# Experts weight their rows by the gates and scatter with addition into one row per token

## The chip, the cores and the metric

The kernel runs on one core of a Trainium2 chip. The metric is the time of one execution on the device, in microseconds (us). The core has five engines that run side by side and wait for each other by semaphores: PE (TensorE, matrix products), DVE (VectorE) and ACT (ScalarE) for work on tiles, POOL (GpSimd), which here also issues the indirect DMAs, and SP, which issues the plain ones. A tile has 128 partitions. All DMAs share the core's 16 DMA engines.

## The reference, cut to what matters

Two layers, each `x = x + s * silu(f)`. The change touches the second layer's f, a mixture of 8 experts of which each token takes 2:

```python
logits = xt @ wg                                   # xt: 8192 tokens x 256
scores = softmax(logits);  topv, topi = top_k(scores, 2)
topv = topv / sum(topv)
pos = running number of each (k, token) within its expert     # k = 0 first
valid = pos < capacity                             # capacity 2 * 8192 / 8 = 2048
gate = topv * valid
disp[topi, pos] = xt                               # the rows of each expert
h = relu(disp @ w1 + b1)                           # 256 -> 1024
y = h @ w2 + b2                                    # 1024 -> 256
f = sum over k of gate[k] * y[topi[k], pos[k]]
x = x + s * silu(f)
```

Everything is f32; in the experts the kernel writes each f32 matrix as a sum of two f16 halves and forms three products for one.

## The kernel before

`program` calls the stages `prepare`, `mix`, `recur`, `attend`, `route`, `experts` and `combine`. Each is a block: all engines begin it together and end it together. Within a block the order on each engine is the order in which its program is written; nothing reorders it.

`recur` also clears the DRAM tensor `expert_rows` (`y_dram`, 2 x 8192 rows of 256 f32, one per chosen expert and token) with 16 DMAs of 1 MB from SP, since a (k, token) beyond an expert's capacity gets no row (L684).

`route` finds the two best experts of each token, their gates (`gates`, 128 x 2 x 64), and each token's place in its expert. A loop of 128 steps on POOL, ACT, DVE and PE (L1236 to L1295) builds the table `token`: for each of the 8 x 2048 places of the experts the number of the (k, token) that stands there, plus one, or 0 for an empty place. From it DVE makes `idx`, the row of x to be gathered (L1251), and `dst`, the row of `expert_rows` to be written (L1248).

`experts` goes through 32 groups of 512 places, four (g = 0 to 3) to an expert. The loop of PE, ACT and DVE holds two experts, that of POOL two groups. In group n:

- PE forms h in eight chunks of six matmuls (L1645 to L1647) into four PSUM buffers; ACT takes them out with relu (L1600), DVE forms the lower halves (L1539). Then PE turns the x of group n+1 (L1617) and forms y in 96 matmuls (L1666 to L1668).
- DVE takes y out of PSUM, scales it and adds b2 into `yo` (L1563), which raises `yb_ready`. PE waits for it before it writes y of the next group. In front of that DVE copies the next group's columns of `dst` into `dcol` (`take_dcol`, L1455), for which it waits until the scatter of the group before has landed (`y_out`).
- POOL issues four indirect DMAs that gather the rows of group n+2 (`gather`, L1426), waits for `yb_ready`, and issues four that scatter `yo` to `expert_rows` (L1438), 128 rows of 1 KB each.
- SP loads the weights of the next expert into `raw`.

`combine` takes 16 tiles of 128 tokens x 4 batches x 256. SP loads the two rows of each token, `ya` and `yb` (L1715), six tiles ahead in eight buffers; ACT multiplies `ya` by the first gate (`first`, four instructions, L1782); DVE adds `yb` times the second gate (`add`, four instructions, L1742), ACT forms silu (L1773), DVE multiplies by s (`prod_st`, L1755), POOL adds x (L1765), SP stores (L1723).

## Time and profile before

| | us |
|---|---|
| median of 3 runs (lowest, highest) | 1655.68 (1654.1, 1657.88) |
| profiled execution, its own time | 1656.6 |
| span of the profile | 1654.8 |
| PE, DVE, ACT, POOL busy | 1321.9, 1069.8, 644.6, 608.4 |
| experts, matmuls of the groups (829 to 1551) | 722 |
| combine (from 1563) | 92 |

The span runs from the first to the last instruction. Busy is the time in which an engine executes an instruction of its own; issuing a DMA counts as busy on POOL and not on SP. A wait is put down to the instruction that released it. The average over the whole span says little here, since the stages have different limits.

### The profile page before, as it was taken

How to read it: one execution, taken by the hardware profiler on the slowest of the kernel's cores; microseconds unless marked ns; L12 is line 12 of the kernel's file. 1: busy time of each engine (PE TensorE's matmuls, PEld its weight loads, DVE VectorE, ACT ScalarE, POOL GpSimd, SP SyncE). 2: the span in 40 equal slices, each digit the busy share in tenths (PEclk: the TensorE clock that was granted, in tenths of full speed). 3: DMA queues.
4: the chain of work that ended last, by engine and by line, in shares of the span. 5: the costliest groups of instructions: out<-in, count | busy, mean ns of one | idle time of the engine just before them, and what ended most of it. 6: DMA issues, size and time to landing. Idle time of an engine off the chain costs nothing. (4 is left out here: it accounts for less than half of the span.)

```text
span 1654.8 us, 23701 instructions
## 1 busy us (share of the span) xinstructions
PE 1321.9 (80%) x7637; PEld 904.2 (55%) x7637; DVE 1069.8 (65%) x2021; ACT 644.6 (39%) x947; POOL 608.4 (37%) x567
## 2 busy tenths in 40 slices
PE   0699999668999898335499999999999999999400
PEld 0466666336777776311156676666667665667300
DVE  0677776016999999789855555665455655555398
ACT  0255554222322222125354544454444455454263
POOL 0112121001666666714423433333433333343245
PEclk9899999658999999655599999999999999999755
DMA  8000000811000001010121313121221313122396
GB/s 262 1 0 0 0 0 0 348 59 39 25 25 25 25 28 37 0 51 0 29 80 52 103 46 100 51 83 55 81 71 47 103 42 103 52 93 46 102 319 222
DMA packets 75222, 116.07 MB, mean 70 GB/s; under 512 B 9313, under 2 KB 62371, under 8 KB 73088
## 3 DMA queue, kind: packets, MB, share of 16 engines
q1 hardware_dynamic: 53520, 72.44, 13.2%
q0 software_dynamic: 12720, 33.96, 6.8%
q10 hardware_dynamic: 8896, 8.53, 1.7%
q8 instruction: 54, 0.88, 0.2%
q14 instruction: 32, 0.26, 0.1%
HBM read 65.36 MB, written 50.33 MB: 70 GB/s over the span
## 5 line engine op out<-in xcount | busy, mean ns | idle before, releaser
L1600 ACT ACTIVATE e_h_all<-e_pH,e_b1c,e_h_scale 128x512 f32<-128x512 f32 x256 | 199.8, 781 | 370.9 <-PE e_pH L1647 370.6
L1666 PE MATMUL e_pY<-e_w_hi,e_h_hi 128*128 128x256 f16 x1024 | 279.3, 273 | 5.2 <-DVE e_w_lo L1511 5.2
L1667 PE MATMUL e_pY<-e_w_lo,e_h_hi 128*128 128x256 f16 x1024 | 279.1, 273 | 0.0
L1668 PE MATMUL e_pY<-e_w_hi,e_h_lo 128*128 128x256 f16 x1024 | 279.1, 273 | 0.0
L1426 POOL DMA_INDIRECT e_xg<-xn_rows,e_icol x136 | 154.4, 1135 | 302.0 <-DVE e_icol L1452 260.2
L1539 DVE TENSOR_TENSOR e_h_lo<-e_h_all,e_h_hi 128x512 f16<-128x512 f32 x256 | 177.2, 692 | 108.1 <-ACT e_h_hi L1600 102.1
L1645 PE MATMUL e_pH<-e_x_hi,e_w_hi 128*128 128x512 f16 x512 | 196.5, 384 | 10.2 <-issue 6.4
L1647 PE MATMUL e_pH<-e_x_hi,e_w_lo 128*128 128x512 f16 x512 | 196.6, 384 | 0.0
L1646 PE MATMUL e_pH<-e_x_lo,e_w_hi 128*128 128x512 f16 x512 | 196.5, 384 | 0.0
L1438 POOL DMA_INDIRECT expert_rows<-e_yo,e_dcol x128 | 130.9, 1023 | 151.7 <-DVE e_yo L1563 120.7
L1563 DVE SCALAR_TENSOR_TENSOR e_yo<-e_pY,e_y_scale,logit_st 128x1024 f32<-128x1024 f32 x32 | 41.1, 1283 | 154.4 <-PE e_pY L1668 154.4
L1085 PE MATMUL c_pY<-wqkv,c_xnT 128*128 128x256 f32 x512 | 130.0, 412 | 0.0
L1085 PEld LDWEIGHTS c_pY<-wqkv,c_xnT 128*128 128x128 f32 x512 | 107.8, 211 | 21.4 <-issue 1.1
L1666 PEld LDWEIGHTS e_pY<-e_w_hi,e_h_hi 128*128 128x128 f16 x1024 | 100.2, 98 | 18.6 <-DVE e_h_lo L1539 7.4
L1668 PEld LDWEIGHTS e_pY<-e_w_hi,e_h_lo 128*128 128x128 f16 x1024 | 100.2, 98 | 11.6
L1667 PEld LDWEIGHTS e_pY<-e_w_lo,e_h_hi 128*128 128x128 f16 x1024 | 100.2, 98 | 11.4
L1600 ACT ACTIVATE e_h_hi<-e_pH,e_b1c,e_h_scale 128x512 f16<-128x512 f32 x128 | 99.0, 774 | 0.0
L1645 PEld LDWEIGHTS e_pH<-e_x_hi,e_w_hi 128*128 128x128 f16 x512 | 50.7, 99 | 69.9 <-issue 14.1
L1295 PE MATMUL d_ptab<-d_val,d_ohl 128*128 128x256 f16 x128 | 44.8, 400 | 51.6 <-ACT d_ohl L1276 26.8
L1647 PEld LDWEIGHTS e_pH<-e_x_hi,e_w_lo 128*128 128x128 f16 x512 | 50.6, 99 | 61.9 <-issue 2.7
L1646 PEld LDWEIGHTS e_pH<-e_x_lo,e_w_hi 128*128 128x128 f16 x512 | 50.6, 99 | 57.6 <-issue 2.8
L999 ACT ACTIVATE c_q<-c_pY 128x1024 f32<-128x1024 f32 x16 | 16.4, 1024 | 151.1 <-DVE c_qk L950 141.1
(257 smaller groups left out, 2554.5 us busy)
## 6 DMA issues: line engine op xcount, KB each, us to landing
raw<-L_ffn_w SPq DMA_DIRECT2D x18, 1024.0 KB, 5.9
expert_rows<-r_zero SPq DMA_DIRECT2D x16, 1024.0 KB, 16.7
x_st<-L_attn_x ACTq DMA_DIRECT2D x4, 2048.0 KB, 22.2
xn_rows<-c_xn SPq DMA_DIRECT2D x16, 512.0 KB, 2.9
f_ya<-expert_rows SPq DMA_DIRECT2D x16, 512.0 KB, 5.7
f_yb<-expert_rows SPq DMA_DIRECT2D x16, 512.0 KB, 6.6
out<-f_ya SPq DMA_DIRECT2D x16, 512.0 KB, 3.7
e_xg<-xn_rows,e_icol POOLq DMA_INDIRECT x136, 2.8
```

The costliest lines, as they stand in the source:

```text
L1085: last = pe.matmul(dst[:, b, :], xnT[:, kk, b * P:(b + 1) * P], v.wqkv[:, kk, n * D:(n + 1) * D], start=False, stop=(kk == KD - 1), skip_g ...
L1295: pe.matmul(ptab[:, 0:2 * P], ohl[m][:, u, :], val[u][:, :, :].rearrange("p a b -> p (a b)"), start=False, stop=False, skip_group_check=Tr ...
L1426: pool.indirect_dma_start(xg[u][:, q, :], None, v.xn3_dram, bass.IndirectOffsetOnAxis(icol[u][:, q:q + 1], axis=0), bounds_check=N - 1, oo ...
L1438: pool.indirect_dma_start(v.y_dram, bass.IndirectOffsetOnAxis(dcol[u][:, q:q + 1], axis=0), yo[u][:, q, :], None, bounds_check=TOPK * N - ...
L1539: dve.tensor_tensor(h_lo[:, h, :], h_all[h % 2][:, :], h_hi[:, h, :], ALU.subtract).then_inc(h_lo_ready, 1)
L1600: last = act.activation(dst, pH[h % NPH][:, :], ACT.Relu, bias=b1c[eu][:, h:h + 1], scale=h_scale[eu][:, 0:1])
L1645: pe.matmul(pH[h % NPH][:, :], w1_hi[:, k, rows], x_hi[:, k, :], start=(k == 0), stop=False)
L1646: pe.matmul(pH[h % NPH][:, :], w1_hi[:, k, rows], x_lo[:, k, :], start=False, stop=False)
L1647: last = pe.matmul(pH[h % NPH][:, :], w1_lo[:, k, rows], x_hi[:, k, :], start=False, stop=(k == KD - 1))
L1666: pe.matmul(pY[:, q, :], h_hi[:, h, cols], w2_hi[:, h, :], start=(h == 0), stop=False)
L1667: pe.matmul(pY[:, q, :], h_hi[:, h, cols], w2_lo[:, h, :], start=False, stop=False)
L1668: last = pe.matmul(pY[:, q, :], h_lo[:, h, cols], w2_hi[:, h, :], start=False, stop=(h == HT - 1))
```

## The change

Each expert multiplies its rows by the gates and adds them into one row per token. `expert_sums` has 8192 rows for the tokens and 2048 more, to which the empty places of an expert go (each to a row of its own within one expert). The gates are turned by PE, written to the DRAM tensor `gate_rows`, and gathered by place with `gid` as the index: 512 single values a group. The scatter adds to what is in the row. Because two experts may add to the same row, POOL waits at the end of each expert until all its scatters have landed. `combine` loads one row per token, and ACT begins with silu. The core of the diff (declarations of buffers and semaphores are left out):

```diff
@@ -71,7 +72,8 @@
     c[:, C_P] = np.arange(P) + 1
     c[NS::GRP, C_SAT] = SAT
     c[:, C_E:C_E + E] = np.arange(E)
-    c[:, C_G:] = np.arange(TOPK * NG)
+    c[:, C_G:C_D] = np.arange(TOPK * NG)
+    c[:, C_D:] = N + np.arange(P)[:, None] + P * (np.arange(P) % (CAP // P))
     return c
 
 
...
-    v.y_dram = nc.dram_tensor("expert_rows", [TOPK * N, D], F32, kind="Internal").ap()
+    v.y_dram = nc.dram_tensor("expert_sums", [N + CAP, D], F32, kind="Internal").ap()
+    v.gate_dram = nc.dram_tensor("gate_rows", [TOPK * N, 1], F32, kind="Internal").ap()
...
-                parts = TOPK * N // (P * 8)
+                parts = (N + CAP) // (P * 8)
...
+                sp.wait_ge(gates_taken, 1)
+                sp.dma_start(v.gate_dram.rearrange("(n p) o -> n (p o)", p=P), gate_rows[:, :]).then_inc(gates_out, 16)
+                sp.wait_ge(gates_out, 16)
...
-                for t in (v.idx, v.dst):
+                for t in (v.idx, v.dst, v.gid):
...
-                linked(dve.tensor_tensor(gates[:, 1, :], ee[:, :], gates[:, 0, :], ALU.mult))
+                dve.tensor_tensor(gates[:, 1, :], ee[:, :], gates[:, 0, :], ALU.mult).then_inc(gates_ready, 1)
...
@@ -1237,18 +1249,21 @@
                                           v.cst[:, bass.ds(C_G + n, 1)], ALU.is_equal, ALU.mult)
                         dve.tensor_scalar(val[u][:, 1, :], iota[:, :], hi[:, bass.ds(n, 1)],
                                           v.cst[:, C_P:C_P + 1], ALU.is_equal, ALU.mult).then_inc(one_ready, 1)
+                dve.wait_ge(gates_turned, 1)
+                dve.tensor_copy(gate_rows[:, :], pgate[:, 0:P]).then_inc(gates_taken, 1)
                 dve.wait_ge(table, 1)
                 linked(dve.tensor_copy(tab[:, :, :], ptab[:, 0:2 * P].rearrange("p (a b) -> p a b", a=2)))
 
                 linked(dve.scalar_tensor_tensor(token[:, :], tab[:, 0, :], float(P), tab[:, 1, :], ALU.mult, ALU.add))
 
-                linked(dve.tensor_scalar(empty[:, :], token[:, :], 0.0, None, ALU.is_equal))
-                linked(dve.scalar_tensor_tensor(t1[:, :], empty[:, :], float(TOPK * N + 1), token[:, :],
-                                                ALU.mult, ALU.add))
-                dve.tensor_scalar(v.dst[:, 0:P], t1[:, :], -1.0, None, ALU.add)
+                dve.tensor_scalar(v.gid[:, 0:P], token[:, :], -1.0, 0.0, ALU.add, ALU.max)
+                linked(dve.scalar_tensor_tensor(empty[:, :], token[:, :], 0.0, v.cst[:, C_D:C_D + P],
+                                                ALU.is_equal, ALU.mult))
                 linked(dve.tensor_scalar(t2[:, :], token[:, :], float(N), float(-N), ALU.is_gt, ALU.mult))
                 linked(dve.scalar_tensor_tensor(t2[:, :], t2[:, :], -1.0, token[:, :], ALU.add, ALU.add))
-                linked(dve.tensor_scalar(v.idx[:, 0:P], t2[:, :], 0.0, None, ALU.max))
+                linked(dve.tensor_scalar(t2[:, :], t2[:, :], 0.0, None, ALU.max))
+                dve.tensor_copy(v.idx[:, 0:P], t2[:, :])
+                linked(dve.tensor_tensor(v.dst[:, 0:P], t2[:, :], empty[:, :], ALU.add))
 
             @block.gpsimd
             def _(pool):
...
+                pe.wait_ge(gates_ready, 1)
+                pe.transpose(pgate[:, 0:P], gates[:, :, :].rearrange("p k g -> p (k g)"), v.ident).then_inc(gates_turned, 1)
...
@@ -1427,20 +1449,37 @@
                                                 bass.IndirectOffsetOnAxis(icol[u][:, q:q + 1], axis=0),
                                                 bounds_check=N - 1, oob_is_err=False).then_inc(x_in[u], 16)
 
+                def gather_gates(n, u):
+                    pool.wait_ge(gcols, n + 1)
+                    pool.sem_inc(passed, 1)
+                    for q in range(BLK):
+                        pool.indirect_dma_start(gate[u][:, q:q + 1], None, v.gate_dram,
+                                                bass.IndirectOffsetOnAxis(gcol[u][:, q:q + 1], axis=0),
+                                                bounds_check=TOPK * N - 1, oob_is_err=False).then_inc(gate_in[u], 16)
+
                 for u in range(2):
                     gather(u, u)
-                with pool.Fori(0, NGR // 2) as i:
-                    for u in range(2):
-                        gather(2 * i + u + 2, u)
-                        pool.wait_ge(yb_ready, 2 * i + u + 1 + 1)
+                gather_gates(0, 0)
+                with pool.Fori(0, E) as e:
+                    for g in range(GRPS):
+                        u = g % 2
+                        n = GRPS * e + g
+                        gather(n + 2, u)
+                        gather_gates(n + 1, 1 - u)
+                        pool.wait_ge(weighted, n + 1)
                         pool.sem_inc(passed, 1)
                         for q in range(BLK):
                             pool.indirect_dma_start(
                                 v.y_dram, bass.IndirectOffsetOnAxis(dcol[u][:, q:q + 1], axis=0), yo[u][:, q, :], None,
-                                bounds_check=TOPK * N - 1, oob_is_err=False).then_inc(y_out[u], 16)
+                                bounds_check=N + CAP - 1, oob_is_err=True, compute_op=ALU.add).then_inc(y_out[u], 16)
+                        if g == GRPS - 1:
+                            for m in range(2):
+                                pool.wait_ge(y_out[m], 8 * BLK * GRPS * (e + 1) + 16 * m)
                 for u in range(2):
                     pool.wait_ge(y_out[u], 16 * BLK * NGR // 2 + 16 * u)
                     pool.wait_ge(x_in[u], 16 * BLK * (NGR // 2 + 1))
+                pool.wait_ge(gate_in[0], 16 * BLK * (NGR // 2 + 1))
+                pool.wait_ge(gate_in[1], 16 * BLK * NGR // 2)
 
             @block.vector
             def _(dve):
...
+                    dve.tensor_copy(gcol[u][:, :], v.gid[:, bass.ts(n, BLK)]).then_inc(gcols, 1)
...
@@ -1563,6 +1603,11 @@
                     dve.scalar_tensor_tensor(yo[u][:, :, :], pY[:, :, :], y_scale[eu][:, 0:1],
                                              b2b[eu].unsqueeze(1).broadcast_to([P, BLK, D]),
                                              ALU.mult, ALU.add).then_inc(yb_ready, 1)
+                    dve.wait_ge(gate_in[u], 8 * BLK * (n - u) + 16 * BLK)
+                    dve.wait_ge(yb_ready, n + 2)
+                    dve.tensor_tensor(yo[u][:, :, :], yo[u][:, :, :],
+                                      gate[u][:, :].unsqueeze(2).broadcast_to([P, BLK, D]),
+                                      ALU.mult).then_inc(weighted, 1)
 
                 groups(dve, body)
 
...
-                rows = v.y_dram.rearrange("(k b t p) d -> t k p b d", k=TOPK, b=B, p=P)
+                rows = v.y_dram[0:N, :].rearrange("(b t p) d -> t p b d", b=B, p=P)
...
-                    for k, y in enumerate((ya[n], yb[n])):
-                        sp.dma_start(y[:, :].rearrange("p (b d) -> p b d", b=B), rows[t, k]).then_inc(y_in[n], 16)
+                    sp.dma_start(ya[n][:, :].rearrange("p (b d) -> p b d", b=B), rows[t]).then_inc(y_in[n], 16)
...
@@ -1731,26 +1772,19 @@
                 for n in range(NB):
                     sp.wait_ge(o_out[n], 16 * (NT // NB) + 16)
 
+            @block.scalar
+            def _(act):
+                def body(i, n, left):
+                    act.wait_ge(y_in[n], 16 * (i + 1))
+                    act.sem_inc(passed, 1)
+                    act.activation(ya[n][:, :], ya[n][:, :], ACT.Silu).then_inc(silu_ready, 1)
+
+                rounds(act, body)
+
             @block.vector
             def _(dve):
-                def add(i, n):
-                    t = NB * i + n
-                    dve.wait_ge(y_in[n], 32 * (i + 1))
-                    dve.wait_ge(first_ready, t + 1)
-                    for b in range(B):
-                        cols = slice(b * D, (b + 1) * D)
-                        last = dve.scalar_tensor_tensor(ya[n][:, cols], yb[n][:, cols],
-                                                        v.gates[:, 1, bass.ds(b * NT + t, 1)], ya[n][:, cols],
-                                                        ALU.mult, ALU.add)
-                    last.then_inc(sum_ready, 1)
-
-                add(0, 0)
-                add(0, 1)
-
                 def body(i, n, left):
                     t = NB * i + n
-                    if left >= 2:
-                        add(i + (n + 2) // NB, (n + 2) % NB)
                     dve.wait_ge(silu_ready, t + 1)
                     dve.tensor_tensor(ya[n][:, :], ya[n][:, :], v.prod_st[:, t, :], ALU.mult).then_inc(sg_ready, 1)
 
...
-            @block.scalar
-            def _(act):
-                def silu(t, n):
-                    act.wait_ge(sum_ready, t + 1)
-                    act.activation(ya[n][:, :], ya[n][:, :], ACT.Silu).then_inc(silu_ready, 1)
-
-                def first(i, n):
...
```

POOL in `experts`, its loop's first group, before (e_xg is the gathered x, expert_rows the destination, e_yo the scaled y):

```order
L1432 ISA
L1426 DMA e_xg<-xn_rows,e_icol 128x256 x4
L1435 REGISTER_ALU
L1438 DMA expert_rows<-e_yo,e_dcol 16384x256 x4
L1423 REGISTER_ALU
L1426 DMA e_xg<-xn_rows,e_icol 128x256 x4
L1438 DMA expert_rows<-e_yo,e_dcol 16384x256 x4
L1432 REGISTER_ALU
L1432 COMPARE_AND_BRANCH
```

And the same place in the changed kernel (e_gate are the gathered gates):

```order
L1448 DMA e_xg<-xn_rows,e_icol 128x256 x4
L1453 REGISTER_ALU
L1456 DMA e_gate<-gate_rows,e_gcol 128x1 x4
L1469 REGISTER_ALU
L1472 DMA expert_sums<-e_yo,e_dcol 10240x256 x4
L1445 REGISTER_ALU
L1448 DMA e_xg<-xn_rows,e_icol 128x256 x4
L1456 DMA e_gate<-gate_rows,e_gcol 128x1 x4
L1472 DMA expert_sums<-e_yo,e_dcol 10240x256 x4
```

Four gathers of gates stand between the gather of rows and the scatter, and the loop now holds four groups.

DVE in `experts`, the end of one group and the beginning of the next, before (e_h_lo is the lower half of h):

```order
L1455 COPY e_dcol<-dst 128x4
L1561 REGISTER_ALU
L1563 SCALAR_TENSOR_TENSOR e_yo<-e_pY,e_y_scale,logit_st 128x1024
L1534 ISA
L1539 TENSOR_TENSOR e_h_lo<-e_h_all,e_h_hi 128x512
L1534 REGISTER_ALU
L1537 CAST e_h_hi<-e_h_all 128x512
```

And in the changed kernel:

```order
L1494 COPY e_dcol<-dst 128x4
L1495 REGISTER_ALU
L1495 COPY e_gcol<-gid 128x4
L1601 REGISTER_ALU
L1603 SCALAR_TENSOR_TENSOR e_yo<-e_pY,e_y_scale,logit_st 128x1024
L1606 REGISTER_ALU
L1608 TENSOR_TENSOR e_yo<-e_yo,e_gate 128x1024
L1574 ISA
L1579 TENSOR_TENSOR e_h_lo<-e_h_all,e_h_hi 128x512
L1574 REGISTER_ALU
L1577 CAST e_h_hi<-e_h_all 128x512
```

A copy stands ahead of the scaling, and the multiplication by the gates between it and the first lower half of the next group.

ACT at the beginning of `combine`, before (f_ya is the loaded tile):

```order
L1782 ACTIVATE f_ya<-f_ya,gates 128x256 x12
L1773 ACT_TABLE_LOAD
L1773 ACTIVATE f_ya<-f_ya 128x1024
L1699 UNCONDITIONAL_BRANCH
L1782 ACTIVATE f_ya<-f_ya,gates 128x256 x4
L1773 ACTIVATE f_ya<-f_ya 128x1024
L1782 ACTIVATE f_ya<-f_ya,gates 128x256 x4
```

And in the changed kernel:

```order
L1741 UNCONDITIONAL_BRANCH
L1780 ACT_TABLE_LOAD
L1780 ACTIVATE f_ya<-f_ya 128x1024 x8
L1741 REGISTER_ALU
L1741 COMPARE_AND_BRANCH
```

The multiplications by the first gate are gone, and silu follows the load of its table.

## Rows read from the trace of the kernel before

**Rows 1.** Stages: us, busy of PE, PEld, DVE, ACT, POOL; clock, DMA share, GB/s

```profile
829.00:1551.00 722.00, 707.16 (x4888) 482.86 (x4888) 408.96 (x689) 341.97 (x488) 271.87 (x253) 0.99 0.24 70
...
1563.00:1655.00 92.00, 0.00 (x0) 0.00 (x0) 73.03 (x80) 43.70 (x81) 40.11 (x16) 0.50 0.86 274
```

**Rows 2.** Waits of PE, 829 to 1552: us in total, times, longest

```profile
PE e_pH L1645 <- issue: 6.4, 3, 2.4
PE e_pY L1666 <- DVE e_w_lo L1511: 5.2, 8, 0.9
```

**Rows 3.** Timeline of combine, one tile: start, us, engine, line, operation

```profile
1612.43 1.21 DVE L1755 TENSOR_TENSOR f_ya<-f_ya,prod_st 128x1024 f32<-128x1024 f32 x1
...
1613.57 3.75 DVE L1742 SCALAR_TENSOR_TENSOR f_ya<-f_yb,gates,f_ya 128x256 f32<-128x256 f32 x4
...
1617.24 1.21 DVE L1755 TENSOR_TENSOR f_ya<-f_ya,prod_st 128x1024 f32<-128x1024 f32 x1
```

**Rows 4.** Stages as in rows 1: a stretch of recur, one of combine

```profile
340.00:345.00 5.00, 5.00 (x12) 2.39 (x10) 0.00 (x0) 0.37 (x1) 0.00 (x0) 0.68 0.00 0
...
1603.00:1613.00 10.00, 0.00 (x0) 0.00 (x0) 10.00 (x11) 5.30 (x10) 4.84 (x2) 0.50 1.03 328
```

**Rows 5.** L1765 and L1755, ns shortest/median/longest; timeline of POOL's last three

```profile
L1765 POOL TENSOR_TENSOR f_ya<-f_ya,x_st x16: 2336/2420/3316, 1579.8 to 1649.1; 128x1024 f32<-128x1024 f32 x16
...
L1755 DVE TENSOR_TENSOR f_ya<-f_ya,prod_st x16: 1210/1211/3354, 1578.4 to 1643.5; 128x1024 f32<-128x1024 f32 x16
...
1642.66 8.73 POOL L1765 TENSOR_TENSOR f_ya<-f_ya,x_st 128x1024 f32<-128x1024 f32 x3 [2.39 <-DVE f_ya L1755]
```

**Rows 6.** Timeline of the head of combine; last, landings of L1715's loads

```profile
1562.66 0.37 SPq L1715 DMA_DIRECT2D f_ya<-expert_rows  x1
...
1568.10 1.70 ACT L1782 ACTIVATE f_ya<-f_ya,gates 128x256 f32<-128x256 f32 x4 [27.61 <-DMA f_yb<-expert_rows]
...
1573.11 1.67 DVE L1742 SCALAR_TENSOR_TENSOR f_ya<-f_yb,gates,f_ya 128x256 f32<-128x256 f32 x4 [1.52 <-ACT f_ya L1782]
...
1576.05 1.28 ACT L1773 ACT_TABLE_LOAD   x1
...
1577.34 1.06 ACT L1773 ACTIVATE f_ya<-f_ya 128x1024 f32<-128x1024 f32 x1
...
1579.85 2.35 POOL L1765 TENSOR_TENSOR f_ya<-f_ya,x_st 128x1024 f32<-128x1024 f32 x1 [24.70 <-DVE f_ya L1755]
...
DMA to landing us min/median/max: 3.9/6.2/9.1
```

**Rows 7.** Timeline of experts between two groups, and at a loop's turn

```profile
1143.03 1.28 DVE L1563 SCALAR_TENSOR_TENSOR e_yo<-e_pY,e_y_scale,logit_st 128x1024 f32<-128x1024 f32 x1 [3.47 <-PE e_pY L1668]
...
1145.81 0.69 DVE L1539 TENSOR_TENSOR e_h_lo<-e_h_all,e_h_hi 128x512 f16<-128x512 f32 x1 [1.49 <-ACT e_h_hi L1600]
...
1147.03 0.78 ACT L1600 ACTIVATE e_h_all<-e_pH,e_b1c,e_h_scale 128x512 f32<-128x512 f32 x1 [0.52 <-PE e_pH L1647]
...
1193.30 0.69 DVE L1539 TENSOR_TENSOR e_h_lo<-e_h_all,e_h_hi 128x512 f16<-128x512 f32 x1 [5.03 <-ACT e_h_hi L1600]
```

**Rows 8.** L1539, L1438 with its landings, L1426: ns shortest/median/longest

```profile
L1539 DVE TENSOR_TENSOR e_h_lo<-e_h_all,e_h_hi x256: 691/692/695, 833.5 to 1538.1; 128x512 f16<-128x512 f32 x128
...
L1438 POOL DMA_INDIRECT expert_rows<-e_yo,e_dcol x128: 982/1000/1240, 856.8 to 1554.2; - x128
...
DMA to landing us min/median/max: 2.2/2.5/6.5
...
L1426 POOL DMA_INDIRECT e_xg<-xn_rows,e_icol x136: 997/1002/3028, 816.5 to 1546.7; - x136
```

**Rows 9.** The last scatter of experts, and the block's end on POOL

```profile
1554.16 0.99 POOL L1438 DMA_INDIRECT expert_rows<-e_yo,e_dcol  x1 [0.30 <-issue]
...
L1383 POOLq DRAIN  x1: 4973/4973/4973, 1556.9 to 1556.9; - x1
```

**Rows 10.** Timeline of DVE at the end of route

```profile
812.08 0.42 DVE L1241 COPY d_tab<-d_ptab 128x256 f32<-128x256 f32 x1 [0.70 <-PE d_ptab L1297]
```

40 lines of the change are left out of this document (15 added, 25 removed).

## The prediction

> **What bounds the kernel now.** I read the table of stages first, then the timeline of the last stage, then the waits and timelines of the expert stage. The reader is to see two different stages. In the expert stage (829 to 1551 us) PE is busy for 707.16 of 722 us [rows 1], and the waits say that it lost 5.2 us to the lower half of W2 in 8 waits and 6.4 us to "issue" in 3 [rows 2]. So PE alone sets these 722 us, 22.6 us for each of 32 groups, and anything put on DVE or POOL there is free until it makes PE wait. In the combining stage (1563 to 1655 us) PE does nothing and DVE is busy for 73.03 of 92 us [rows 1]. There one tile follows the other every 4.81 us (1612.43 to 1617.24): 3.75 us of L1742 (four instructions) and 1.21 us of L1755, with no idle time, while POOL's addition of 2.42 us (the median in rows 5) fits beside them [rows 3]. The four L1742 need 3.75 us only because POOL runs at the same time: the ones of 1573.11, without POOL, took 1.67 us for four [rows 6]. ACT and DMA are below that, DMA not by much: 328 GB/s at a share of 1.03 [rows 4].
>
> **The combining stage.** Before, a tile loads two times 512 KB and stores 512 KB. The change loads 512 KB once, and takes four ACT copies (L1782), four DVE instructions (L1742) and one wait pair away. What is left of a tile is ACT 1.06, DVE 1.21, POOL at least 2.34 us. The first question is what DVE and POOL cost together, because the rows say that they exclude each other: L1765 has 2336 ns at least and 3316 at most, L1755 has 1210 and 3354 [rows 5]. The last three additions of POOL are the pattern that the change gives to the whole stage, since there DVE has only L1755 left: 8.73 us for three, 3.15, then 3.3, and about 2.3 for the one that has no DVE beside it [rows 5]. I take 3.3 us a tile: POOL 2.15 with the port, DVE 1.15 with it. Sixteen tiles: 3.15 + 14 x 3.3 + 2.34 = 51.7 us, against 71.5 us from POOL's first start at 1579.85 to the end of the last three, 1642.66 + 8.73 = 1651.39 [rows 5, 6]. Gain 19.8 us.
>
> Second, the head. Before, POOL starts 17.2 us after the first load is issued (1562.66 to 1579.85) [rows 6]: the tile's pair of loads is there after 5.4, three rounds of copies, the table load (1.28) and silu (1.06) follow. After, there is load, table load, silu, L1755's multiplication, addition. One load lands before the pair does; I take 4.4 us, between L1715's shortest landing of 3.9 and the 5.4 of the pair [rows 6]. 4.4 + 0.1 + 1.28 + 1.06 + 0.1 + 1.15 + 0.2 = 8.3 us. Gain 8.9 us. The table load could lie under the load of the tile (another 1.3 us), but it stands after the wait in ACT's order before, so I do not count on it. The tail (last store, 3.4 us) stays.
>
> Third, what is late next. DMA has 16 x 1.05 = 16.8 MB to move instead of 25.2. At 328 GB/s [rows 4] a tile of 1.05 MB is 3.2 us, only 0.1 under the 3.3 of DVE and POOL. So DMA does not decide if its rate holds, and the period cannot fall below 3.2 us whatever DVE and POOL do: at best 1.6 us more gain. If mixed loads and stores of this kind run only at 300 GB/s, 3.5 us a tile and 3.2 us less gain. Sum of the stage: -28.7 us (bounds -30 and -25).
>
> **The expert stage.** Added on DVE for each group: the weighting of yo, a tensor_tensor of 128x1024 f32 like L1755, 1.21 us, and a copy of gcol (0.16 us, in the idle time before yo). Where it stands: yo is done at 1143.03 + 1.28 = 1144.31, and the next instruction, the first lower half of the next group, starts at 1145.81 after 1.49 us of idle time, waiting for ACT [rows 7]. The weighting with its wait for DVE's own result ends at 1144.31 + 0.04 + 1.21 = 1145.56: it fits, with 0.25 us left. Of the 31 gaps 28 are 1.4 to 1.5 us like this one, and three, where the loop turns, 3.6 to 5.03, the longest ahead of 1193.30 [rows 7]. If the cover is gone, there is a second one: ACT takes that lower half only at its third chunk, which starts at 1147.03 after 0.52 us of waiting for PE [rows 7], and PE is four buffers ahead of ACT. So up to about 0.8 us of lateness costs nothing. Could the weighting be slower than its row? Beside POOL's DMA issues L1539, also with two inputs in SBUF, keeps 691 to 695 ns over 256 executions [rows 8], so POOL's issuing does not slow DVE, and the scatters wait for the weighting anyway. I take 0. The bound on the other side is the contended multiplication of 3.35 us [rows 5]: 3.35 + 0.04 - 1.49 - 0.8 = 1.1 us a group, 31 groups, 34 us.
>
> Because yb_ready is raised before the weighting, PE's wait for its PSUM tile is not moved; only POOL's scatter is, by 1.25 us.
>
> Added on POOL for each group: four gathers of single gates. POOL issued 8 indirect DMAs a group, 1.0 us and 0.3 us of issue each [rows 8, 9]; now it is 12, 15.7 us of 22.6. What stands behind them on POOL is the scatter of the group. It has 6.9 us of spare time a group, so the four accumulating scatters may be 1.7 us slower each (3.0 instead of 1.3) before POOL sets the pace. At the end of each expert POOL also waits for all its scatters to land, about 2.5 us [rows 8], seven times inside the stage; behind that wait stands the gather of rows that PE needs a whole group later, some 13 us after it is issued. Hidden. DVE's take_dcol waits for the scatter of the group before, over 10 us after it was issued. Hidden. I take 0 for both.
>
> What an accumulating DMA costs no row shows. From below it is a plain scatter, landing 2.5 us [rows 8]. Since the sum has to be read, added and written, I take one more memory trip, half of another landing, 1.2 us, and as upper bound the longest landing of the row, 6.5 us, so 4 us more. The issue on POOL I take as the row has it, 1.0 us, because it is nearest in kind; the upper bound is the longest indirect DMA of the trace, 3.03 us [rows 8]. The Trainium skill, page "DMA: Bandwidth & Descriptors", section "Rules for kernel authors", says that an accumulating DMA reads its destination and writes it later with nothing holding the bytes in between; no row here shows such a DMA. By that rule a scatter costs a read and a write one after the other, up to a second landing, and by the plain scatter's row nothing more; it speaks against the change at the tail and at the turns of an expert, and stands behind the rival of a late landing below.
>
> The tail of the stage is exposed: the last weighting, +1.25, and the slower landing, +1.2, ahead of POOL's drain of 4.97 us, which I leave as it is [rows 9]. Sum +2.4 (bounds +1.2 and +6). At the head of the stage one copy more stands before the largest value: +0.2.
>
> **Route and the rest.** In route the copy of the turned gates falls into the 0.7 us in which DVE waits for the table [rows 10]. Behind the copy of the table DVE has 7 small instructions over 128x128 instead of 6 after token, each under the 0.42 us of that copy of twice the size [rows 10]: +0.3. The gates' rows are written by one DMA of 64 KB issued at about 811.8; with a landing like the scatter's 2.5 us [rows 8] it is there at 814.5, beside the end of DVE: +0.2, at worst +2. Constants: 64 KB more at the start, at about 300 GB/s +0.2. The clearing shrinks from 16 to 10 MB, but it was already over at 340 us, with PE busy in the sweeps for all of 340 to 345 us and DMA at 0 [rows 4]: 0.
>
> **Sum.** -28.7 + 2.4 + 0.2 + 0.3 + 0.2 + 0.2 = -25.4 us. The profiled execution took 1656.6 us, so it comes to 1631.2; the median of the three runs is 1655.68, 0.9 lower, which gives 1630.3. I say 1631.
>
> **The rivals.**
> - DMA binds the combining stage at a lower rate. For it: the share is already 1.03 [rows 4]. Against it: 4.81 us per tile was held by DVE without idle time, so the rate was not tested beyond 328 GB/s. At 280 GB/s 3.75 us a tile, +7 us: 1638.
> - The accumulate lands late (10 us and more). Against it nothing but the kind. It shows at the seven turns of an expert and in the tail; at 10 us more in the tail and 1 us a turn: 1646.
> - DVE and POOL do not alternate strictly; then DMA's 3.2 us and the earlier table load decide: 1628.
> - The other side: POOL becomes the bound of the expert stage. Its place is the issue of the accumulating scatters. At the trace's longest 3.03 + 0.3 us each, POOL has 8 x 1.3 + 4 x 3.33 = 23.7 us a group, 1.1 more than 22.6; 35 us in 32 groups: 1666. It begins to cost at 3.0 us an issue, and the gain is used up at 3.2 us (25 us over 128 issues, 0.2 us each, above the 3.0).
> - The weighting is not covered, by the contended price: 1631 + 34 = 1665; at half of that overhang 1648. Against it L1539's even 692 ns. The Trainium skill, page "SBUF — State Buffer", section "Who interferes with whom", says that a DVE instruction with two SBUF inputs contends with a GpSimd instruction that reads SBUF, and that the loser waits for the whole of it; if the issue of an indirect DMA counted as one, a weighting would wait for up to one issue, and the even 692 ns speak against that.
> - That the change does not do what it says: the second load is gone from the code, so the traffic falls in any case; only the period could stay with POOL. That is no case of its own: 4.8 us a tile would need another 1.5 us from somewhere, for which no row speaks.
>
> **How the numbers follow.** A measurement of this kernel can tell about 0.2% (3.3 us) from no change. Forecast (1626 to 1635) 0.60; DMA at a lower rate 0.14; not strictly alternating 0.09; accumulate late 0.08; POOL bound 0.05; weighting exposed 0.04. Nearly all of the first four and half of the last are faster: faster 0.93, same 0.02, slower 0.05. The range takes in the bounds of the combining stage and of the tail and most of the second rival: 1625 to 1641.
>
> **What would show it.** Additions of POOL at 3.3 us each with multiplications of DVE between them, POOL's first one about 8 us after the first load, no ACT copies, a stage of some 63 to 64 us. In the expert stage a DVE tensor_tensor of 1.2 us right behind yo, the gap behind it near 0.2 us, PE's waits as before, yo to yo still 22.6 us, POOL's accumulating issues near 1.0 us. It is wrong if PE waits for x or yo in the expert stage, if POOL is busy without gaps there, or if the tiles of the last stage stand further apart than 3.5 us.

## The result, and the profile after

| kernel, session | this, us | kernel before beside it, us | ratio, 95% interval |
|---|---|---|---|
| changed, first measured (4 runs) | 1713.65 | 1656.78 | 1.034 [1.031, 1.037] |
| changed, again, on chip 5 (2 runs) | 1682.46 | 1659.56 | 1.014 [1.008, 1.021] |
| changed, again, on chip 14 (4 runs) | 1636.53 | 1656.74 | 0.988 [0.985, 0.990] |
| changed, again, on chip 5, later (4 runs) | 1635.13 | 1653.85 | 0.987 [0.984, 0.990] |

The result that answers the prediction is the first row: 57 us slower, 83 us above the 1631 that I gave. The other rows are the same program word for word. I call kernels that ran together, one after the other on one chip, a session. The kernel before of the first row is four runs, three of which were made before the prediction. Each row agrees within itself to 8 us, and the kernel before is within 6 us of itself in all four; the changed kernel moves by 78. Most of what follows is about that. First the profiled execution of the first row (1709.59 us, span 1707.4). Its stages, in the columns of [rows 1], and its waits on PE and DVE in 829 to 1624 us (us in total, times, longest):

```profile
829.00:1624.00 795.00, 722.23 (x4888) 476.49 (x4888) 450.85 (x753) 339.51 (x488) 497.95 (x382) 0.99 0.34 65
...
1645.00:1707.00 62.00, 0.00 (x0) 0.00 (x0) 48.30 (x16) 17.99 (x17) 51.38 (x16) 0.50 0.85 271
```
```profile
PE e_pH L1690 <- ACT e_h_hi L1645: 35.2, 41, 2.1
PE e_pY L1711 <- DVE e_h_lo L1579: 12.7, 24, 0.7
PE e_pY L1711 <- DVE e_w_lo L1551: 11.3, 14, 1.4
PE e_pH L1690 <- issue: 8.0, 8, 2.3
...
DVE e_yo L1603 <- remote: 209.4, 23, 12.9
...
DVE e_yo L1603 <- PE e_pY L1713: 30.2, 7, 4.6
```

The last stage is what was predicted. The expert stage takes 795 us where it took 722, with the same 4888 matmuls. PE now waits for ACT and DVE in a stage where it had waited for 15.4 us in all, the 6.4 and 5.2 us of [rows 2] and this one:

```profile
PE e_pH L1645 <- DVE e_x_lo L1518: 3.8, 1, 3.8
```

DVE's own wait ahead of yo is put down to "remote" 23 times: the profile found no instruction on the core whose end released it. The timeline of one such place, between two groups (start, us, engine, line, operation; in brackets the idle time before):

```profile
1177.90 0.27 PE L1713 MATMUL e_pY<-e_w_hi,e_h_lo 128*128 128x256 f16 x1
...
1178.44 0.38 PE L1692 MATMUL e_pH<-e_x_hi,e_w_lo 128*128 128x512 f16 x1
...
1181.17 1.00 POOL L1456 DMA_INDIRECT e_gate<-gate_rows,e_gcol  x1 [0.30 <-issue]
...
1183.08 0.38 PE L1692 MATMUL e_pH<-e_x_hi,e_w_lo 128*128 128x512 f16 x1
1183.54 1.28 DVE L1603 SCALAR_TENSOR_TENSOR e_yo<-e_pY,e_y_scale,logit_st 128x1024 f32<-128x1024 f32 x1 [7.92 <-remote]
1183.62 0.78 ACT L1645 ACTIVATE e_h_all<-e_pH,e_b1c,e_h_scale 128x512 f32<-128x512 f32 x1 [14.25 <-PE e_pH L1692]
```

PE's last matmul of the group ends at 1178.17, and yo waits for nothing but its increment of y_done. DVE is idle, yet starts at 1183.54, 5.4 us late. ACT waits for the first chunk of the next group, which is done at 1179.47, and starts at 1183.62 too. The record of semaphore updates in the same trace has y_done at 1183.52, and the increments of h_done of four chunks, done at 1179.47, 1180.87, 1182.17 and 1183.46, all from 1183.59 on. So the work was done and its increments came late, together, 1.35 us after the issue of the last gate gather (1181.17 + 1.00) ended, which is about when that gather lands (its packets end by 1183.26 in the trace). Over the whole stage most of PE's increments beside L1456 are late by more than 0.1 us (112 of 128), by 2 to 3 us on average; beside the accumulating scatters nearly all are on time. In the kernel before all are 0.01 to 0.02 us. The numbers for the lateness are approximate: this trace and those of e5 to e12 lack 6 to 48 of PE's 339 updates of the stage, so which update belongs to which matmul is not always certain; other ways to pair them give 0.3 us less to 0.9 us more. A measure that needs no pairing is the time from the end of PE's last matmul of a group to the start of DVE's yo: 3.52 us on average over the 32 groups, 0.05 in the kernel before.

Only PE's increments are late. No update of ACT or DVE in this stage stands more than 0.02 us behind its instruction, and DVE's `e_h_lo`, where it waited for ACT, starts 0.03 us (median) after ACT's end.

The same place in the profiled execution on chip 14, and DVE's waits there in 829 to 1624 us:

```profile
1146.30 0.27 PE L1713 MATMUL e_pY<-e_w_hi,e_h_lo 128*128 128x256 f16 x1
...
1146.61 1.29 DVE L1603 SCALAR_TENSOR_TENSOR e_yo<-e_pY,e_y_scale,logit_st 128x1024 f32<-128x1024 f32 x1 [3.36 <-PE e_pY L1713]
...
1147.48 1.00 POOL L1456 DMA_INDIRECT e_gate<-gate_rows,e_gcol  x1 [0.30 <-issue]
```
```profile
DVE e_yo L1603 <- PE e_pY L1713: 150.9, 32, 7.8
```

The gathers are issued at nearly the same point as there (from 1144.87 on, 1.7 us ahead of PE's end; there 0.9), yo starts 0.04 us after PE's end, and no wait is "remote". The term by term account of both, each from one profiled execution:

| part | before | first session | chip 14 | predicted change | change on chip 14 |
|---|---|---|---|---|---|
| start to first yo | 854.58 | 859.80 | 856.21 | +0.9 | +1.6 |
| first yo to last yo | 693.48 | 760.97 | 693.81 | 0 | +0.3 |
| last yo to first load of combine | 14.60 | 23.88 | 22.74 | +2.4 | +8.1 |
| from there to the end | 92.14 | 62.75 | 62.54 | -28.7 | -29.6 |
| span | 1654.8 | 1707.4 | 1635.3 | -25.4 | -19.5 |

The combining stage, answering to [rows 3, 5, 6]: durations ns shortest/median/longest of the first session, and the first loads and the first addition in its timeline:

```profile
L1799 POOL TENSOR_TENSOR f_ya<-f_ya,x_st x16: 2336/3317/3322, 1652.6 to 1701.7; 128x1024 f32<-128x1024 f32 x16
...
L1789 DVE TENSOR_TENSOR f_ya<-f_ya,prod_st x16: 1219/3358/3368, 1651.2 to 1696.2; 128x1024 f32<-128x1024 f32 x16
```
```profile
1644.65 4.39 SPq L1756 DMA_DIRECT2D f_ya<-expert_sums  x6
...
1652.63 9.71 POOL L1799 TENSOR_TENSOR f_ya<-f_ya,x_st 128x1024 f32<-128x1024 f32 x3 [18.22 <-DVE f_ya L1789]
```

Head 8.0 us (8.3 predicted), additions at 3.3 us each, 51.4 us from the first start to the last end (51.7 predicted). The tail of the expert stage, same execution, answers to [rows 9]:

```profile
1620.77 1.28 DVE L1603 SCALAR_TENSOR_TENSOR e_yo<-e_pY,e_y_scale,logit_st 128x1024 f32<-128x1024 f32 x1 [4.02 <-issue]
1621.43 1.00 POOL L1456 DMA_INDIRECT e_gate<-gate_rows,e_gcol  x1 [0.30 <-issue]
1622.17 1.23 DVE L1608 TENSOR_TENSOR e_yo<-e_yo,e_gate 128x1024 f32<-128x1024 f32 x1
...
1625.87 1.00 POOL L1456 DMA_INDIRECT e_gate<-gate_rows,e_gcol  x1 [0.30 <-issue]
1627.18 1.63 POOL L1472 DMA_INDIRECT expert_sums<-e_yo,e_dcol  x1 [0.30 <-issue]
...
1632.86 1.55 POOL L1472 DMA_INDIRECT expert_sums<-e_yo,e_dcol  x1 [0.30 <-issue]
```
```profile
L1405 POOLq DRAIN  x1: 6765/6765/6765, 1637.1 to 1637.1; - x1
```

The weighting ends at 1623.40, but the scatters start at 1627.18, behind four gate gathers for a group that does not exist. Each scatter's issue takes 1.6 us and not 1.0, and POOL's drain 6.77 us and not 4.97.

### The profile page after: what moved, and what is told of

Same layout as the page of the kernel before. It is cut to its first block and busy times, and to the rows that moved or that the text cites. A ratio compares the mean times of both kernels' runs of the same rounds, so it can differ in the third digit from the quotient of the medians.

```text
span 1707.4 us, 23984 instructions
## 1 busy us (share of the span) xinstructions
PE 1337.1 (78%) x7638; PEld 898.1 (53%) x7638; DVE 1087.5 (64%) x2025; ACT 616.6 (36%) x883; POOL 851.2 (50%) x699
## 5 line engine op out<-in xcount | busy, mean ns | idle before, releaser
L1472 POOL DMA_INDIRECT expert_sums<-e_yo,e_dcol x128 | 222.8, 1741 | 136.9 <-DVE e_yo L1608 104.9
L1448 POOL DMA_INDIRECT e_xg<-xn_rows,e_icol x136 | 154.4, 1135 | 124.4 <-DVE e_icol L1491 78.3
L1456 POOL DMA_INDIRECT e_gate<-gate_rows,e_gcol x132 | 139.5, 1057 | 40.3 <-issue 40.3
## 6 DMA issues: line engine op xcount, KB each, us to landing
x_st<-L_attn_x ACTq DMA_DIRECT2D x4, 2048.0 KB, 22.4
```

The source lines that it names most:

```text
L1448: pool.indirect_dma_start(xg[u][:, q, :], None, v.xn3_dram, bass.IndirectOffsetOnAxis(icol[u][:, q:q + 1], axis=0), bounds_check=N - 1, oo ...
L1456: pool.indirect_dma_start(gate[u][:, q:q + 1], None, v.gate_dram, bass.IndirectOffsetOnAxis(gcol[u][:, q:q + 1], axis=0), bounds_check=TOP ...
L1472: pool.indirect_dma_start(v.y_dram, bass.IndirectOffsetOnAxis(dcol[u][:, q:q + 1], axis=0), yo[u][:, q, :], None, bounds_check=N + CAP - 1 ...
```

## The experiments

They ran in five sessions: e1 to e4 on chip 9, e5 to e8 on chip 15, e9 to e12 on chip 5, e13 to e16 on chip 14, e17 and e18 on chip 5 again. The kernel before ran in each (1656.73, 1657.26, 1659.56, 1656.74, 1653.85). "Late" is how long after the end of PE's matmul its increment stands in the record of updates, between 1000 and 1400 us, with the uncertainty named above. A session in which increments are late is called held.

**e1, no gate gathers.** The gates are a constant 0.5, set once.

```diff
-                    for q in range(BLK):
-                        pool.indirect_dma_start(gate[u][:, q:q + 1], None, v.gate_dram, ...)
+                    (nothing)
```

> The changed kernel without its 132 gathers of gates; the gate tile is a constant 0.5, so the outputs carry no gates; the weighting, the accumulating scatters and the combining stage stay. Theory (the gathers of single 4-byte values hold back the semaphore increments of PE, ACT and DVE while they are in flight; in the profile of the change 112 of 128 PE increments beside them are over 0.1 us late, 2.1 us on average): PE's increments are 0.01 to 0.02 us behind their matmul again, yo to yo is 22.4 us on average, and the time is 1655.7 - 29.4 (combining) + 6 (tail) = 1630 to 1640 us. Rival (the accumulating scatters, 1.64 us each on POOL instead of 1.0, set the pace): over 1690 us.

1632.51 (4 runs), 0.986 [0.982, 0.989], increments 0.01 us late. I read it as "only the gathers are left". It does not show that: e2 to e4, in the same session, have small gathers and no late increment either, so e1 against the first session compares two occasions as well as two programs. What it shows is that the rest of the change works without a loss in the groups (yo to yo 22.31 us).

**e2, four 4-byte gathers a group added to the kernel before**, their values go nowhere.

```diff
+                        gather_gates(2 * i + u + 1, 1 - u)   # wide[u][:, q, 0:1] <- xn_rows, by token index
```

> The kernel before with four gathers of 4 bytes x 128 added to each group at the place where the change has them; their values are not used. Theory of the held increments: the expert stage grows by 65 to 80 us as in the change, 1720 to 1735 us. Rival (the loss needs the accumulating scatters or the weighting beside the gathers): at most 1670 us, since POOL has the room for four more issues of 1.3 us.

1663.34 (10 runs), 1.004 [1.002, 1.006], on time. I took "small gathers hold increments" as refuted. That was too quick, as e10 shows.

**e3 and e4, two gathers a group in the changed kernel**, of 4 and of 512 bytes, from the normalised rows; gates 0.5.

```diff
-                    for q in range(BLK):
+                    for q in range(2):
```

> The changed kernel with two gathers of 4 bytes x 128 a group instead of four, gates a constant 0.5. Theory of the held increments: they are held for about 2.6 us less in each group, so yo to yo falls from 24.9 to about 22.6 to 23.5 us and the time to 1635 to 1665 us. Rival (a cost for each indirect DMA whatever its size): halfway, 1670 us.

> As the run with two gathers a group, but each gathers 512 bytes x 128 instead of 4 bytes x 128, gates a constant 0.5. If small elements are what holds the increments: PE's increments are on time, 1630 to 1640 us. If it is the number of indirect DMAs or of descriptors: the same time as with two gathers of 4 bytes, and the same late increments.

1629.99 and 1629.43 (one run each), on time; e3 is below both of its ranges. With the first session's 1713.65 in mind it looked as if the number of gathers, their source or their destination decided. The next four varied these.

**e5 to e8.** e5 is e3 with four gathers in place of two. The others change one line of the changed kernel:

```diff
-                        pool.indirect_dma_start(gate[u][:, q:q + 1], None, v.gate_dram,
+                        pool.indirect_dma_start(gate[u][:, q:q + 1], None, v.xn3_dram.rearrange("n (d o) -> (n d) o", o=1),   # e6
-                                bounds_check=N + CAP - 1, oob_is_err=True, compute_op=ALU.add)
+                                bounds_check=N + CAP - 1, oob_is_err=False)   # e7
-                    for q in range(BLK):
+                    for q in range(2):   # e8, gates 0.5
```

> The changed kernel with its four 4-byte gathers per group kept, but read from the normalised token rows by the token index (a 4-byte piece of a row) into a tile that nobody reads; the gates are a constant 0.5, so the output's weights are left out. Theory A (it takes four small gathers together with the accumulating scatters): increments of TensorE again some 2 us late beside the gathers, yo to yo 24 to 25 us, 1700 to 1720 us. Theory B (it is the small gates tensor or its index that does it): increments on time (0.02 us), yo to yo 22.2 to 22.5 us, 1630 to 1645 us.

> The changed kernel, whose four gate gathers per group keep their index and destination but read single values of the normalised token rows in place of the gates; the weights that it applies are wrong values for that reason. Theory B1 (the small gates tensor as the source does it): increments on time, yo to yo 22.2 to 22.5 us, 1630 to 1645 us. Theory B2 (destination tile or index list, or four gathers beside accumulation, whatever the source): as the changed kernel, 1705 to 1720 us.

> The changed kernel with a plain scatter in place of the accumulating one, so a token's row holds one expert's part and not the sum. Theory A (gathers together with accumulation): increments on time, 1625 to 1640 us. Theory B (the gate gathers alone, whatever the scatter): increments still late beside the gathers, yo to yo 24 to 25 us, 1695 to 1715 us (the scatter's issue some 0.6 us shorter per instruction).

> The changed kernel with two of its four gate gathers per group, same source, index and destination; the gates that weight the rows are a constant 0.5, so the output's weights are left out. Theory A (four small gathers in a row needed): increments on time, 1628 to 1640 us. Theory B (each gate gather holds increments until it lands): half of the lateness, yo to yo 23 to 23.7 us, 1660 to 1685 us.

| | us (2 runs each) | ratio, 95% interval | late beside the small gathers, mean, and how many over 0.1 us |
|---|---|---|---|
| e5 | 1719.33 | 1.038 [1.035, 1.041] | 2.12, 60 of 66 |
| e6 | 1711.72 | 1.033 [1.029, 1.038] | 2.18, 56 of 66 |
| e7 | 1728.53 | 1.044 [1.039, 1.049] | 2.17, 53 of 58 |
| e8 | 1643.08 | 0.992 [0.989, 0.995] | 1.64, 27 of 31 |

e8 lies between its two ranges, e7 13 us above its own. Source, index, destination and the kind of scatter make no difference to the lateness beside the small gathers. But e8 holds increments and e3 does not, and the two differ in nothing but source, index and destination, which e5 and e6 had just ruled out. The traces of e5 to e8 had one more thing in common with the first session, and e1 to e4 had not: of the landings of the row gathers (L1448) most were missing from the record, 708 of 2176 there in e8 against all but 3 in e3, from the first gathers of the stage on, before any gate gather ran. The page hints at it: in held sessions it has no landing time for these gathers, in the others it has one (2.9 us on chip 14) except in e1 and e15. So it was not the program that differed, but the occasion. e9 to e12 test that.

**e9 to e11: earlier kernels again, together.** e9 is the changed kernel, e10 is e2, e11 is e3, not a letter changed. **e12** moves the gate gathers behind the scatters:

```diff
                         gather(n + 2, u)
-                        gather_gates(n + 1, 1 - u)
                         pool.wait_ge(weighted, n + 1)
                         ... (the four scatters)
+                        gather_gates(n + 1, 1 - u)
```

> The changed kernel again, word for word, together with a repeat of two earlier kernels on one chip. Theory C (what holds increments is a property of the chip that the kernel ran on, since the runs with increments on time were all on one chip and those with late ones on others): as slow or as fast as the other two of this call are, 1705 to 1720 us on a chip that holds increments, 1630 to 1650 us on one that doesn't. Theory P (it belongs to the program): 1705 to 1720 us on every chip.

> The kernel before with four 4-byte gathers added per group (their values go nowhere), again. Theory C: increments of TensorE late beside the small gathers if the changed kernel's are in this call, 1690 to 1735 us; else as in its first run, 1660 to 1666 us. Theory P: 1660 to 1666 us and on time, whatever the changed kernel does.

> The changed kernel with two 4-byte gathers per group from the normalised rows, gates a constant 0.5 (weights left out), again. Theory C: with late increments as the run with two gate gathers had, 1640 to 1646 us, if the changed kernel is slow in this call; 1628 to 1632 us if not. Theory P: 1628 to 1632 us.

> The changed kernel with the four gate gathers of the next group behind the scatters of this one in place of ahead of them (everything is computed). If the hold needs plain indirect transfers in an unbroken row (eight in a row in the changed kernel, eight here too: four gates, then four rows of the next group but one), the time stays 1700 to 1720 us; if what costs is that the hold falls on the increments of the last matmuls of a group, its place moves by the four scatters (7 us) and the time is 1640 to 1690 us.

| | us (runs) | ratio, 95% interval | late beside the small gathers |
|---|---|---|---|
| e9 | 1682.46 (2) | 1.014 [1.008, 1.021] | 1.68, 51 of 66 |
| e10 | 1743.32 (2) | 1.051 [1.043, 1.059] | 2.44, 55 of 60 |
| e11 | 1632.62 (2) | 0.984 [0.978, 0.991] | 0.83, 25 of 37 |
| e12 | 1670.93 (4) | 1.009 [1.006, 1.013] | beside the row gathers that follow them: 1.57, 33 of 42 |

e10 decides it: the kernel that took 1663.34 on chip 9 takes 1743.32 here, while the kernel before beside it moves by 3 us. DVE's waits ahead of yo, e2 first, then e10:

```profile
DVE e_yo L1580 <- PE e_pY L1686: 152.1, 32, 7.6
```
```profile
DVE e_yo L1580 <- remote: 206.7, 24, 12.3
...
DVE e_yo L1580 <- PE e_pY L1686: 28.3, 6, 5.2
```

Theory P falls, and e2's reading with it. Theory C has the direction right and not the sizes: e9 and e11 are faster than it says, e10 slower. e11 shows the size of the harm: its increments are late as well, by less than 1 us on average, and it still takes 1632.62; two gathers nearly stay within the cover that PE, ACT and DVE have of each other (yo to yo 22.27 us; 22.76 in e8). In e12 the late increments moved to where the row gathers come, and 12 us came back of e9's 1682.46.

The traces of e10 and e12 say more. A small gather does not always hold increments, and not only small gathers have late ones beside them. In e12, beside the gate gathers, which follow the accumulating scatters as first to fourth of a row of plain transfers, none of 9 increments is late; beside the 1 KB row gathers that follow them without a pause, as fifth to eighth, about 3 in 4 are. In e10 the plain scatters of 1 KB rows sometimes follow a pause of POOL and sometimes the eight gathers directly. As first to fourth after a pause (over 1 us without an issue) at most one of 87 increments beside them is late; as ninth to twelfth all of 25 are, by about 4 us on average. One such place:

```profile
1031.01 1.03 POOL L1452 DMA_INDIRECT expert_rows<-e_yo,e_dcol  x1 [0.30 <-issue]
...
1034.94 0.98 POOL L1452 DMA_INDIRECT expert_rows<-e_yo,e_dcol  x1 [0.30 <-issue]
```
```profile
1036.08 0.78 ACT L1618 ACTIVATE e_h_all<-e_pH,e_b1c,e_h_scale 128x512 f32<-128x512 f32 x1 [4.54 <-PE e_pH L1665]
```

ACT's chunk was done on PE at 1031.09, and the last gather's issue had ended at 1030.71; the increment came at 1036.05. Over all nine held traces PE's increments are at most 0.2 us late on average beside the first four plain transfers of a row, and some 1 to 4 us beside the places behind them, row gathers, small gathers and scatters alike. But a long row is not enough either: each held trace begins the stage with eight to twelve plain transfers in a row, the first eight of them row gathers, and the few increments beside the fifth and later of these (one or two a trace) are on time. The kernel before has 63 rows of four, each behind a pause, and that one long row at the start, which fits its steady time in held sessions.

**e13 to e16.** e13 is the changed kernel, e14 is e1. e15 and e16 break the row of eight plain transfers (four row gathers, four gate gathers), and compute everything:

```diff
+                        pool.wait_ge(x_in[u], 8 * BLK * (n - u) + 32 * BLK)   # e15
                         gather_gates(n + 1, 1 - u)
```
```diff
-                        gather_gates(n + 1, 1 - u)
                         ...
                                 bounds_check=N + CAP - 1, oob_is_err=True, compute_op=ALU.add).then_inc(y_out[u], 16)
+                            gather_gates(n + 1, 1 - u, [q])   # e16: one gather behind each scatter
```

> The changed kernel word for word, as the yardstick of this chip: 1680 to 1716 us if the chip holds increments, 1630 to 1650 us if it doesn't.

> The changed kernel without the gate gathers (gates a constant 0.5, the output's weights left out), again, beside the changed kernel. Theory R (a row of more than four plain indirect transfers is what holds increments): four row gathers between slow accumulating scatters hold nearly nothing, 1628 to 1640 us on every chip. Theory G (each plain gather holds them on a chip that holds at all): 1645 to 1670 us if the changed kernel is at 1680 to 1716 us.

> The changed kernel in which GpSimd waits for the landing of its four row gathers (some 1.6 us) before it issues the four gate gathers; everything is computed. Theory R: the row of eight becomes two rows of four, increments at most 0.3 us late on average, 1630 to 1650 us. Theory G: unchanged, 1680 to 1720 us on a chip that holds increments.

> The changed kernel with one gate gather behind each accumulating scatter in place of four behind the row gathers; everything is computed. Theory R: no row longer than five plain transfers, increments on time, 1630 to 1645 us on every chip. Theory G: late beside each gather, 1660 to 1710 us on a chip that holds increments.

1636.53 (0.988 [0.985, 0.990]), 1631.24 (0.984 [0.982, 0.986]), 1677.24 (1.011 [1.009, 1.013]) and 1638.78 (0.990 [0.987, 0.992]), 4 runs each. On this occasion none of the four has a late increment, so they do not decide between theories R and G. What it does tell is the price of the change without the disturbance: -20.2 us for the whole, of which the gate gathers take 5.3 back (e13 against e14), 3.5 of it in the tail (22.74 us from the last yo to the first load, 19.27 in e14). And e15 lies outside the 1630 to 1650 us of theory R, for another reason (G's condition, a held session, was not met). Its waits of POOL in 829 to 1660 us, and DVE's line on its page:

```profile
POOL e_gate L1456 <- DMA e_xg<-xn_rows,e_icol: 101.9, 29, 6.7
```
```profile
L1495 DVE COPY e_dcol<-dst 128x4 int32 (+1 forms) x33 | 8.6, 260 | 197.0 <-DMA expert_sums<-e_yo,e_dcol 196.7
```

The added wait costs POOL 3.5 us each of 29 times; DVE's copy of the next indices then waits 196.7 us in all for scatters to land, and with it comes everything DVE does. Yo to yo is 23.5 us on average, not 22.4. In e13 POOL had idle time for a new icol of 100.1 us in the whole stage, 3 us a group, and that is all the room there is.

**e17 and e18**, e16 and the changed kernel again, on chip 5.

> One gate gather behind each accumulating scatter, again, for a chip that holds increments. On such a chip (fewer than half of the landings of the row gathers in the trace): theory R (a row of more than four or five plain transfers) 1630 to 1650 us and TensorE's increments under 0.3 us late on average; theory G (each small gather) 1660 to 1700 us, 1 to 2 us late. On a chip that holds none: as before, 1636 to 1644 us, and the two stay untold.

> The changed kernel word for word beside it: 1680 to 1716 us on a chip that holds increments, 1634 to 1640 us on one that holds none.

1638.82 (0.989 [0.986, 0.992]) and 1635.13 (0.987 [0.984, 0.990]), all landings recorded, no late increment. The chip that held increments in e9 to e12 holds none here, so it is no fixed property of the chip. What sets it was not found.

**What stays open.** (1) What differs between sessions: three held increments, three did not, and within each all kernels with small gathers agreed. (2) Why increments are late beside the fifth and later plain transfers of a row. The places in e10's and e12's traces speak against theory G, in which each gather holds them, and the long row at the start of the stage against theory R, in which the length alone does; every later row of more than four has small gathers in it, so their part can't be told from the length. e15 and e16, which shorten the rows, met no held session. The times of the held sessions order by the length of the row: of six 1632.62 and 1643.08, of eight 1670.93 to 1719.33, of up to twelve 1728.53 and 1743.32; they are from different sessions and that is no proof. (3) Whether the kernel before has late increments in a held session: it was not profiled in one; its time doesn't show any. (4) No version that computes everything beats both kernels on every occasion; e16 equals the changed kernel within 4 us where nothing is held, and was not measured where something is. (5) Whether the recording of the profile takes part. Every execution of the changed kernel on record has a span and a granted clock from the profiler, and held sessions lose records of it; no run without the profiler shows whether the increments are late there too.

## Why the prediction was wrong, step by step

- **The combining stage: right.** -28.7 predicted, -29.4 in the first session and -29.6 on chip 14. The mutual exclusion of DVE and POOL at 3.3 us a tile holds over 14 tiles (3317 ns median on POOL). DMA moved 261 GB/s at a share of 0.85 in 1655 to 1665 us of the first session and 315 GB/s at 1.00 in 1590 to 1600 us on chip 14; POOL was busy for all 10 us of both, and for 51.38 us in the stage of both.
- **The weighting: right.** One row on chip 14 has all 32 of them, right behind yo, and none waited:

```profile
L1608 DVE TENSOR_TENSOR e_yo<-e_yo,e_gate x32: 1224/1225/1228, 857.6 to 1551.4; 128x1024 f32<-128x1024 f32 x32
```

  DVE's yo to yo is 22.38 us on average there, 22.37 before. The even 692 ns [rows 8] was a good witness that POOL's issues don't slow a DVE instruction with two inputs, and the rule of the Trainium skill, page "SBUF — State Buffer", section "Who interferes with whom", that the prediction weighed against it did not reach this pair: 1228 ns is the longest of the 32, beside POOL's issues or not.
- **"Added on POOL for each group: four gathers of single gates ... I take 0": the step that failed.** I priced the gathers by what they take of POOL's time (5.2 us a group, which leaves 6.9 to spare) and by who waits for them. In the first session they cost 67.5 us between the first and the last yo, on instructions that neither issue them nor wait for them, by delaying the increments of PE that DVE and ACT wait for. That it is the gathers is shown by e10 against the kernel before, which differ in them, one copy and one wait (7 us in all in e2) and ran together (1743.32 against 1659.56), and by e5 and e6 against e8, together again (four against two, 76 and 69 us); that it needs the occasion as well, by e10 against e2. With them POOL's rows of plain transfers have eight in place of four; whether it is that length or what is in it stays open. No row of before could show it: its eight plain indirect DMAs a group come in two rows of four with a pause between, and no increment is late. The sign that I had named, PE waiting in the expert stage, did come. None of my rivals named it, and the range left no room for a cost of a kind that isn't in the trace.
- **The accumulating scatter: landing right, issue mis-sized.** The row of L1472 on chip 14, with its landings:

```profile
L1472 POOL DMA_INDIRECT expert_sums<-e_yo,e_dcol x128: 1551/1658/2150, 860.0 to 1560.9; - x128
...
DMA to landing us min/median/max: 3.7/3.9/5.4
```

  The landing is 1.4 us above the 2.5 of [rows 8], where I took 1.2 more; its longest is below the plain one's. The rule of the Trainium skill (page "DMA: Bandwidth & Descriptors", section "Rules for kernel authors") of a read and then a write, which I priced at up to a second landing, comes to about half of one. The issue is 1.66 us and not 1.0; four of them fit into POOL's spare time (2.6 of 6.9 us), so it cost only in the tail. POOL did not become the bound, but e15 shows how near it is.
- **The tail: +8.1 on chip 14 where I had +2.4 (bounds 1.2 to 6).** The scatters start 5.24 us after yo's start and not 2.17, since the gate gathers stand ahead of them (+3.1; the weighting alone, e14, makes it +1.3); the four scatters take 7.23 us from first start to last end, not 4.92 (+2.3); from there to the first load 10.27 and not 7.51 (+2.8), of which 1.8 is POOL's drain, which I had left as it is [rows 9]. I named the instructions that the gathers stand ahead of, in the running stage where it is hidden, and did not carry that to the last group where nothing hides it.
- **Route and the head: +0.9 predicted, +1.6 on chip 14, too small to judge.** The copy of the gates (812.34) falls into the wait for the table, as predicted; the table itself comes later (813.12 and not 812.08 [rows 10]) because the loop ahead of it ends about 1 us later. The first yo starts at 856.21 there, at 854.97 in e18 and at 859.80 in the first session, the same program, so this term is below what moves between executions.

Without the late increments the profiled execution took 1637.5 us against 1631.2 predicted. Of these 6.3 us the tail is 5.7, the head 0.7 and the periods 0.3; the last stage gave 0.9 more than predicted, which offsets a part; 0.4 lies outside the span. 1637.5 is inside the range, but it is not what was measured first, and the chance of 0.05 for slower was far too small.

## What to carry to other kernels

Price an added DMA not only by its issue and its landing but by what else runs on the core while it is in flight: compare, for the waits that matter, the end of the releasing instruction with the start of the waiting one, and take a wait put down to "remote" on an idle engine as a sign of a late increment. Look also at how many indirect DMAs GpSimd issues without a pause; here the late increments stood beside the fifth and later of such a row. Repeat a surprising kernel word for word on another occasion before reasoning from its difference to a third; two single sessions led me from a right suspicion to a false refutation (e2), and to a proof that was none (e1). And whatever is issued one group ahead is issued once too often at the end: there it stands on the path.

## What the runs showed of the hardware

- Increments of semaphores by PE arrived late in three of six sessions, by up to 5.4 us, while GpSimd had a row of more than four plain indirect DMAs in flight, and were let go in quick succession 1.0 to 1.4 us (medians of the nine traces) after the issue of the row's last one. Beside the first four of a row they were at most 0.2 us late on average, and beside the long row at the start of the stage on time. Those of ACT and DVE were never more than 0.03 us late. The changed kernel and those of e2 and e3, word for word, had all of them 0.01 to 0.02 us late in the other sessions, e2 with rows of twelve. The changed kernel's time moved between 1635 and 1714 us by it. In held sessions most landing records of plain indirect transfers are missing from the trace (of the row gathers' 2176, 636 to 1042 are there; in the others 2163 or more), which tells the two apart at a glance.
- An accumulating indirect scatter of 128 rows of 1 KB takes 1.55 to 2.15 us of POOL's time (1.66 median), the plain one 1.00, and lands after 3.9 us against 2.5.
- POOL's drain at the end of the block has one length for each program, the same to the nanosecond in every session, and differs between programs: 3.58 us with two small gathers a group (e3, e4, e8, e11), 4.97 with none (before, e1, e14), 5.83 in e16, 6.77 in the changed kernel and in e5, e6, e12 and e15, 9.22 with four beside plain scatters (e2, e7, e10).
